# High part of the next input rows from the PSUM bank by ScalarE instead of a VectorE cast, in a float32 transformer block with experts

## The reference

```python
shift = silu(t) @ W_ada.T + b_ada
h = _ln(x, ln1_g, ln1_b) + shift                 # layer norm of the input rows
qkv = (h @ Wqkv.T).reshape(b, n, 3, H, HD)       # 16 heads of 64
q = _ln(q, qn_g, qn_b); k = _ln(k, kn_g, kn_b)   # per head
attn = softmax(q @ k.T / sqrt(64)); o = attn @ v
x = x + o @ Wout.T
gate = softmax(x @ Wgate.T)                      # 8 experts
# each expert takes its 512 best rows: layer norm, 256 -> 1024, gelu, 1024 -> 256, times gate, added to the row
```

## Time and profile before

| | us |
|---|---|
| median of 3 runs | 1145.9 (1145.66 to 1146.66) |
| the profiled execution | 1148.38 |
| its span, from the first to the last instruction | 1146.6 |

### The profile page before, as it was taken

One profiled execution on the slowest core, in us unless ns is written; L12 is line 12 of the kernel. 1 busy time (PEld: TensorE's weight loads), 2 busy tenths in 40 slices (PEclk: granted clock), 3 DMA queues, 4 the chain that ended last, 5 costly groups with the idle time before them and its releaser, 6 DMA issues.

```text
span 1146.6 us, 24665 instructions
## 1 busy us (share of the span) xinstructions
PE 1097.8 (96%) x8063; PEld 863.1 (75%) x8070; DVE 907.1 (79%) x1693; ACT 728.9 (64%) x1991; POOL 626.1 (55%) x656
## 2 busy tenths in 40 slices
PE   8899999999999999999999999999988789999996
PEld 6677778777777777777777777777765258889985
DVE  6888887888888888888888888888766867777773
ACT  5767777777777777777767777777763224455441
POOL 2566666666656665656666575666662032553432
PEclk9999999999999999999999999999989999999998
DMA  5000000000001000000000010000002314554422
GB/s 184 19 11 20 19 20 19 18 18 18 18 21 34 18 18 18 18 18 18 18 18 18 18 34 21 18 10 19 11 19 111 107 26 149 154 132 115 110 29 28
DMA packets 31775, 48.62 MB, mean 42 GB/s; under 512 B 7920, under 2 KB 28528, under 8 KB 30448
## 3 DMA queue, kind: packets, MB, share of 16 engines
q1 hardware_dynamic: 25584, 39.49, 10.7%
q0 software_dynamic: 6144, 8.52, 4.1%
HBM read 35.29 MB, written 12.71 MB: 42 GB/s over the span
## 4 chain that ended last, share of the span: by engine, by line
PE 35%; issue 25%; POOL 24%; DVE 7%; ACT 6%; POOLq 1%; DMA 1%; ACTq 0%; DVEq 0%; SPq 0%
POOL prob L1062 10%; POOL qk_lo L1075 9%; PE ch L508 5%; PE ch L509 5%; PE ch L510 5%; PE av L1699 3%; POOL qn L967 3%; PE sc L1598 2%; PE mx L1644 2%; ACT prob L1173 2%; DVE m L1481 2%; PE sc L508 1%; PE sc L510 1%; PE sc L509 1%; ACT raw L1128 1%
## 5 line engine op out<-in xcount | busy, mean ns | idle before, releaser
L1062 POOL TENSOR_TENSOR prob<-prob,inverse 128x512 f32<-128x512 f32 x254 | 263.1, 1057 | 229.4 <-DVE inverse L1402 229.4
L1173 ACT ACTIVATE prob<-sc,m 128x256 f32<-128x256 f32 x512 | 235.8, 475 | 127.2 <-DVE m L1481 124.1
L1423 DVE COPY probT<-mx 128x1024 f32<-128x1024 f32 (+1 forms) x128 | 155.3, 1213 | 59.1 <-PE mx L1644 59.1
L1075 POOL TENSOR_TENSOR qk_lo<-qkT,qk_hi 128x512 fp32r<-128x512 f32 x128 | 171.9, 1343 | 29.3 <-ACT qk_hi L1155 29.2
L1481 DVE TENSOR_REDUCE m<-sc 128x4 f32<-128x1024 f32 x127 | 154.4, 1215 | 35.2 <-PE sc L1598 33.9
L508 PE MATMUL ch<-w_hi,hT_lo 128*128 128x512 f32 x384 | 169.9, 443 | 2.2 <-DVE hT_lo L1335 1.8
L509 PE MATMUL ch<-w_lo,hT_hi 128*128 128x512 f32 x384 | 151.7, 395 | 0.0
L510 PE MATMUL ch<-w_hi,hT_hi 128*128 128x512 f32 x384 | 151.4, 394 | 0.0
L1644 PE MATMUL mx<-con,prob 128*128 128x128 f32 x1024 | 140.0, 276 | 10.7 <-POOL prob L1062 10.6
L1699 PE MATMUL av<-probT,V 128*64 128x256 f32 x1024 | 139.6, 394 | 3.5 <-DVE probT L1423 2.7
L1644 PEld LDWEIGHTS mx<-con,prob 128*128 128x128 f32 x1024 | 117.1, 141 | 31.3 <-POOL prob L1062 15.2
(11 more groups left out here) (226 smaller groups left out, 2699.8 us busy)
## 6 DMA issues: line engine op xcount, KB each, us to landing
fcw<-experts SPq DMA_DIRECT2D x8, 2048.0 KB
x_sb<-x SPq DMA_DIRECT2D x16, 256.0 KB, 2.8
xr_sb<-x SPq DMA_DIRECT2D x16, 256.0 KB, 2.8
out<-tok SPq DMA_DIRECT2D x16, 256.0 KB, 2.2
rows_dram<-xh SPq DMA_DIRECT2D x16, 256.0 KB, 2.2
prob<-w_qk SPq DMA_DIRECT2D x2, 512.0 KB, 7.0
qn<-w_qk SPq DMA_DIRECT2D x2, 512.0 KB, 7.4
V<-w_vT SPq DMA_DIRECT2D x2, 512.0 KB, 7.1
```

The source lines that it names most:

```text
L1062: nc.gpsimd.tensor_tensor(pr, pr, r, ALU.mult).then_inc(normalised, 1)
L1075: nc.gpsimd.tensor_tensor(qk_lo[par][:, :], qkT[par][:, :], qk_hi[par][:, :].bitcast(F32), ALU.subtract).then_inc(lo_ready, 1)
L1173: ins = nc.scalar.activation(prob[hp % 2][:, g * N:(g + 1) * N], sc[:, g * N:(g + 1) * N], ACT.Exp, bias=m[hp % 2][:, g:g + 1], scale=-1.0 ...
L1423: nc.vector.tensor_copy(probT[:, 0:half], mx[:, 0:half]).then_inc(probT_ready, 1)
```

## The change

ACT writes both `hT_hi` and `hT` from the bank, half by half, so `shifted_rows` has four instructions instead of two, of the same form but for the output type. DVE's cast is gone, and with it its wait on the chain semaphore. The subtraction is what it was, and stands directly behind the wait for ACT.

```diff
                 for c in range(DC):
                     bias = (bias1[:, c, b + 1:b + 2] if isinstance(b, int) else bias1[:, c, bass.ds(b + 1, 1)])
-                    ins = nc.scalar.activation(hT[:, c, :], bank[:, c * N:(c + 1) * N], ACT.Identity,
-                                               bias=bias, scale=vec[:, LN1_G + c:LN1_G + c + 1])
+                    for dst in (hT_hi, hT):
+                        ins = nc.scalar.activation(dst[:, c, :], bank[:, c * N:(c + 1) * N], ACT.Identity,
+                                                   bias=bias, scale=vec[:, LN1_G + c:LN1_G + c + 1])
                 ins.then_inc(act_read, 1)
...
                 need(act_read, through("act", b, (1, 2)))
-                chain(nc.vector.tensor_copy(hT_hi[:, :, :], hT[:, :, :]))
                 nc.vector.tensor_tensor(hT_lo[:, :, :], hT[:, :, :], hT_hi[:, :, :].bitcast(F32), ALU.subtract).then_inc(hT_split, 1)
...
-            per = 5
+            per = 4
```

## The result

Over 18 runs of each, the median went from 1145.93 to 1148.80 us. The ratio is 1.0023, with a 95% interval of 1.0016 to 1.0029, or 1.8 to 3.3 us. The change makes the kernel slower. The forecast was 1149.7, +3.8 us.

A forecast was written before the change was run, and what follows sets the result against it. The prediction took PE to bound the kernel, slack lying in its wait for POOL's L1062. Terms 3.9 + 0.8 - 0.9 = +3.8 us on the median of 1145.9 gave 1149.7 us, range 1145.2 to 1151.3.

The forecast's parts named there:

- Where the bound is: Attention loop: PE sets the time; of its 0.62 us idle per batch, 0.56 is one wait for POOL's L1062.
- Part of it comes back: Rival, attention loop: PE catches up half of each late start, giving 1147.8 us; chance 0.14.
- hT_lo takes the cast's place, and is longer: Loop: hT_lo, 0.69 us against the cast's 0.41, holds POOL's second product 0.28 longer per batch, +3.9 us in all.
- DVE is first: Loop: DVE's hT_lo is issued at 363.64, 0.05 us ahead of POOL's second product, in all batches.
- the one that starts first wins: Overlapping DVE and POOL instructions: the first runs at full speed, the other is held until 0.14 us before its end.
- POOL gets in first: Rival, loop: POOL's second product is not held, PE's wait falls from 0.56 to 0.34, 1142.7 us; chance 0.11.
- It decides from a shift of 0.05 us on: Loop: the subtraction ready 0.05 us later would let POOL's second product go first and reverse the sign.
- ACT is covered: Loop: ACT's 0.91 us more fits in idle time of 0.49 and 1.34 us, so it costs nothing.
- The rival's price was wrong: Rival that ACT becomes the bound: 1.4 us in all per 0.1 us past its cover, 1152 or more; chance 0.05.
- The entry: Start of the kernel, once: hT and ACT's later work come 0.91 us later, costing +0.8 us.
- Batch 0: First batch, once: without the cast hT_lo ends earlier and PE doesn't wait for it, -0.9 us.
- The sum: Whole kernel: loop 3.9, entry 0.8 and first batch -0.9 give +3.8 us, 1149.7 on the median.

The follow-up runs named there:

- e2: The kernel before with only DVE's part of the change, no cast behind the entry (timing only, high parts wrong); ratio 1.0020.
- e3: The changed kernel with the subtraction split into two halves of 128x256; batch 52.85 us, ratio 1.0005 to the kernel before.
- e4: The changed kernel with `o_lo`, one input in PSUM, moved ahead of the subtraction; batch 52.60 us, ratio 0.9966 to the kernel before.
- e12: The changed kernel with two idle reciprocals of 128x4 on DVE ahead of the subtraction; batch 52.54 us, ratio 0.9946 to the kernel before.
- e10: The changed kernel with one idle reciprocal of 128x4 on DVE ahead of the subtraction, batches 1 to 14; batch 53.09 us, ratio 1.0033 to before.
- e1: The kernel before with only ACT's part, two more instructions writing a spare tile, DVE's cast kept; batch 52.83 us, ratio 1.0007.
- e11: The kernel before with six more ACT instructions behind its two of hT, behind the entry; batch 52.86 us, ratio 1.0004.
- e5: The changed kernel with `o_lo` ahead of the subtraction and the old cast in the entry alone; batch 52.61 us, ratio 0.9953 to before.
- e7: The changed kernel with an idle 128x1 memset on DVE between reduction and subtraction; batch 53.03 us, ratio 1.0008 to the kernel before.

## Why the prediction was right or wrong, step by step

- **Where the bound is.** Right. PE's busy time per batch stayed (52.22 and 52.23), and the batch grew by what the one wait grew, 0.28 and 0.27. Nothing of it came back: the second four transposes start 0.28 later from each batch to the next, 14 times (within 0.02). So the rival "Part of it comes back" is out. DVE's idle time per batch, given as 8 us, is 8.7 by the earlier trace rows; nothing hangs on it.
- **hT_lo takes the cast's place, and is longer.** Right, in sign and size. The term was 14 x 0.28 = 3.9. In batch 14, the last of them, the second four transposes start at 790.11 instead of 787.64, so 2.47 later; behind the hT_lo chunks of batch 0 PE was 1.45 earlier (L1699 at 55.51 instead of 56.96). That is 3.92 over 14 batches. e2 shows that this half of the change is enough for it, e3 that it is the length of the DVE instruction ahead of POOL's product which counts, and not the amount of data, and e4 and e12 that without a holder ahead of it the loss is a gain.
- **DVE is first.** Right, but the reason was too simple. It was argued from recorded starts with a margin of 0.05 us. e10 shows that DVE would still have had the port 0.04 behind, and e12 that it loses at 0.11. The rule "the one that starts first wins" is wrong as a rule on recorded starts. At 0.05 us ahead it gives the same answer as the turning point that was found, so the sign is not luck, but the reason given for it does not hold in general. The real margin was 0.09 to 0.16 us, so the rival "POOL gets in first" was further away than the 0.05 us by which its chance was set. "It decides from a shift of 0.05 us on" was wrong: in e10 the shift is 0.09 and DVE still has the port. The rival's price was right: where POOL is first (e4, e12) the wait is 0.34, as computed.
- **ACT is covered.** Right (e1). The sizes were a little off: the first exponential waits 0.30 less, 1.04 instead of 1.34, where `o_hi` and what follows were forecast 0.42 late. The prediction's list of what the profile would show has this wait at about 1.3, which doesn't fit its own 0.42. The rival's price was wrong (e11): 0.85 us late on ACT cost 0.02 us per batch.
- **The entry.** +0.8 was forecast, and +0.67 is seen at the third chunk, with +0.73 some rows further on (PE's L510 at 17.26 instead of 17.37, with the 0.84 taken off). Part of it can be taken back (e5).
- **Batch 0.** -0.9 was forecast, with -0.95 as the far bound, and it is -1.34. This is the term that was mis-sized, by 0.44. PE's wait was read as 0.95 in the idle column, but the end of the matmuls ahead of it is modelled. Before the change the transposes start at 47.24 and are recorded as 0.60 long, and the chunk starts at 48.80, 1.56 us later; after it, it is 47.14 and 47.49, only 0.35, so the next product can start before the recorded end of the four. So 1.21 us were to be had. Another 0.15 comes at L1699 behind it: PE waited there for DVE's `probT` (0.30 in the row above), and DVE is earlier now.
- **The sum.** By the traces it is 0.73 - 1.34 + 3.92 = +3.3 us, against +3.8 forecast; the runs show +2.9 between the medians and 1.8 to 3.3 by the interval. With the 0.84 by which the weights landed earlier taken off again, the +3.3 is also the 2.4 us by which the spans of the two profiles differ (1146.6 and 1149.0), so little is left for the rest of the kernel. Of the 0.5 us between the forecast and the traces, 0.44 is batch 0. What is left to the medians, 0.4 us, lies within the interval.

## What to carry to other kernels

An instruction that is taken away also moves up all that stood behind it. Where instructions of DVE and POOL overlap in a trace, read for each pair which one is held and for how long, because the shorter of two blockers may be the better one to have in front of the other engine's critical instruction. A change that is a loss in one order can be a gain in another: here the same edit is +0.2% as it stands and, with one unrelated instruction moved ahead, -0.3%, so the order of the neighbours belongs into the test of such a change.

## What the runs showed that was not expected

- Who gets the port isn't decided by the order of the recorded starts alone. Against L1062, hT_lo wins at 0.04 us behind and loses at 0.11 behind. Against another instruction of POOL, the `qn` product at hp = 6, the turning point is nearer. Over the traces of all 14 kernels, DVE's product starts 0.02 to 0.04 behind it 131 times and is held 128 times (the earlier trace rows show one). At 0.00 or 0.01 behind, 37 times, it is POOL's that is held 36 times. Why the point differs between the two was not tried.
- Idle time in front of a matmul is understated. The view gave 0.95 us where 1.21 could be gained. The difference of 0.26 is about what the recorded length of the transposes ahead of it (0.60) is over the 0.35 at which the next product can follow, so differences of starts are the safer reading.
- The kernels with idle work on DVE have batches 0.1 us shorter than the waits explain: e7 has 53.03 us with a wait of 0.84, and the changed kernel 53.12 with 0.83, PE's busy time being 52.12 against 52.23. In the traces of e7, e10 and e12 the meeting of the two `qn` products at hp = 6 also goes the other way: in e7 both start at 386.47, and POOL's takes 1.58 instead of 1.05. But the gain doesn't come at that one place. Counted from the first row of the batch's transposed input, PE is in e7 0.03 us behind the changed kernel at the second four transposes, 0.04 ahead just before that meeting (the product with `o_lo` starts at 26.41 instead of 26.45), and 0.10 ahead at the end of the batch, gained in steps of a few hundredths. The cause stays open.
